# A twelve-layer decoder in one launch: how the attention scores are laid out for the array, who spreads the heads, and two rewritten engine orders

## The reference

```python
x = _layernorm(x + _L0_attn_ref(x, ...))      # linear attention, 16 heads of 8
x = _layernorm(x + _L0_xattn_ref(x, ctx, ...))  # softmax over context and own tokens, 16 heads of 8
x = _layernorm(x + _L0_ffn_ref(x, ...))       # 8 experts and a shared one, SwiGLU
x = _layernorm(x + _L1_attn_ref(x, ...))      # linear attention with decay
x = _layernorm(x + _L1_xattn_ref(x, ctx, ...))  # softmax, 16 heads of 64
x = _layernorm(x + _L1_ffn_ref(x, ...))       # 8 experts, GELU
x = _layernorm(x + _L2_attn_ref(x, ...))
x = _layernorm(x + _L2_xattn_ref(x, ctx, ctx, ...))  # softmax, 16 heads of 8
x = _layernorm(x + _L2_ffn_ref(x, ...))
x = _layernorm(x + _L3_attn_ref(x, ...))      # causal softmax over a latent of 64, 16 heads
x = _layernorm(x + _L3_xattn_ref(x, ctx, ctx, ...))  # mLSTM, 8 heads of 16
x = _layernorm(x + _L3_ffn_ref(x, ...))       # ternary weights
```

## Time and profile before

| | us |
|---|---|
| median of 3 runs | 1021.25 |
| the runs | 1021.25 to 1021.33 |
| the profiled execution, its own time | 1022.06 |
| its span | 1020.0 |
| mean granted clock of TensorE | 0.952 of full speed |

### The profile page before, as it was taken

One profiled execution on the slowest core, in us unless ns is written; L12 is line 12 of the kernel. 1 busy time (PEld: TensorE's weight loads), 2 busy tenths in 40 slices (PEclk: granted clock), 3 DMA queues, 4 the chain that ended last, 5 costly groups with the idle time before them and its releaser, 6 DMA issues. The chain is left out here.

```text
span 1020.0 us, 22561 instructions
## 1 busy us (share of the span) xinstructions
PE 904.2 (89%) x9368; PEld 700.2 (69%) x9368; DVE 539.7 (53%) x1569; ACT 450.7 (44%) x923; POOL 50.8 (5%) x71
## 2 busy tenths in 40 slices
PE   7689899999989998997987979989998989899772
PEld 5257768778778785666556757867887868686441
DVE  5733565653265575347636853655325547454345
ACT  2044343453454673574255233244465446433442
POOL 2300000010010000001000000001001000000000
PEclk8799989999999998999999999999999999999965
DMA  9100000401000301103000000040000030000000
GB/s 344 40 2 3 1 1 1 166 2 37 2 19 1 141 3 40 43 12 139 2 12 1 2 1 2 2 166 33 6 1 19 1 140 1 2 1 2 2 1 21
DMA packets 6838, 36.12 MB, mean 35 GB/s; under 512 B 721, under 2 KB 4305, under 8 KB 5458
## 3 DMA queue, kind: packets, MB, share of 16 engines
q1 hardware_dynamic: 6738, 34.68, 9.1%
HBM read 34.15 MB, written 0.52 MB: 34 GB/s over the span
## 5 line engine op out<-in xcount | busy, mean ns | idle before, releaser
L673 PE MATMUL bank<-xT,weights_F 128*128 128x256 f32 x832 | 202.9, 386 | 3.1 <-ACT p L1818 2.6
L673 PEld LDWEIGHTS bank<-xT,weights_F 128*128 128x128 f32 x832 | 152.0, 193 | 26.8 <-issue 4.2
L681 PEld LDWEIGHTS bank<-weights_F,p 128*128 128x128 f32 x1088 | 133.4, 191 | 18.8 <-DVE p L1363 7.2
L681 PE MATMUL bank<-weights_F,p 128*128 128x128 f32 x1088 | 141.3, 278 | 3.7 <-DVE p L1363 3.0
L1743 ACT ACTIVATE p<-bank 128x512 f32<-128x512 f32 x160 | 84.5, 601 | 121.0 <-PE bank L492 120.9
L1683 ACT ACT_TABLE_LOAD x76 | 97.5, 1283 | 12.9 <-DMA weights_con<-in_con 5.9
L1347 DVE SCALAR_TENSOR_TENSOR res<-bank,comb,res 128x128 f32<-128x128 f32 x184 | 55.7, 345 | 74.1 <-PE bank L681 71.6
L1184 DVE TENSOR_REDUCE m_wide<-bank 128x4 f32<-128x512 f32 x96 | 60.3, 684 | 43.4 <-PE bank L780 33.5
L1818 ACT ACTIVATE p<-bank 128x512 f32<-128x512 f32 x72 | 42.5, 597 | 91.6 <-PE bank L673 91.2
L1363 DVE TENSOR_TENSOR p<-p,bank 128x512 f32<-128x512 f32 x72 | 49.3, 685 | 47.5 <-PE bank L673 27.3
L1894 ACT ACTIVATE p<-bank 128x512 f32<-128x512 f32 x64 | 36.6, 598 | 51.3 <-PE bank L673 51.2
(11 more groups left out here) (319 smaller groups left out, 1356.0 us busy)
## 6 DMA issues: line engine op xcount, KB each, us to landing
weights_F<-in_L1f SPq DMA_DIRECT2D x2, 4096.0 KB, 13.8
weights_F<-in_L0f SPq DMA_DIRECT2D x2, 3456.0 KB, 13.4
weights_F<-in_L2f SPq DMA_DIRECT2D x2, 3456.0 KB, 12.1
weights_Y<-in_L1x_kv SPq DMA_DIRECT2D x2, 1024.0 KB, 10.6
weights_Z<-in_L1x SPq DMA_DIRECT2D x2, 1024.0 KB, 12.9
weights_Y<-in_L2a SPq DMA_DIRECT2D x2, 898.0 KB, 4.4
weights_Z<-in_L2x SPq DMA_DIRECT2D x2, 449.0 KB, 3.2
weights_L3m<-in_L3m SPq DMA_DIRECT2D x2, 288.0 KB, 6.1
```

The source lines that it names most:

```text
L673: m = mm(b[:, k * NT:(k + 1) * NT], W[weight][:, f:f + P], s.xT[:], start=True, stop=True)
L681: m = mm(b[:, tk(u)], h[:, tk(u)], w, start=k == 0, stop=k == len(chunks) - 1)
```

## The change

It has six parts.

1. `bd_k` is gone, and `bd_c` in L0x. The untransposed scores take `bd_q` as weights and the plain keys as the moving side: sixteen products of 32 rows by 128 columns in place of four by 512. DVE's spreading of keys goes from L0a's tail, L0x and L2a; `bd_q` is now made before the first scores of L0x and L2x.
2. In `scores8_t` and L3a's `scores_t` the masks come ahead of the scores.
3. In L1x the maxima are laid out so that a product of 64 rows subtracts them (constant `pick64`).
4. In L3x GpSimd spreads the context `ctxT` into `bd_c`, in L3a already, and the scores take `bd_c` as weights and `xT` as the moving side, eight products of 128 columns in place of two of 512.
5. In L3x PE adds the input gate's term too, by eight more products a call of `units` (constant `choose`, `gates[2]` as the weights), and ACT takes one exponential of 512 columns a bank.
6. `TURN_ORDER` is new on all five engines.

```diff
@@ TURN_ORDER
-        "a15 b1 a3 b2 a1 b1 a1 b1 a1 b2 a1 b2 a3 b2 a7 b2 a1 b1 a2 b1 a5 b1 a1 b2 a1 b1 a1 b3 a1 b2 a1 b3 a1 b1 "
+        "a3 b1 a3 b2 a4 b11 a7 b1 a3 b1 a5 b1 a1 b2 a1 b1 a1 b2 a1 b2 a1 b3 a2 b2 a1 b2 a1 b2 a1 b1 a2 b5 a1 b2 "
...
@@ scores8
-                    for i, b in enumerate(banks):
-                        filled(mm(heads(b[:], 4), s.qT[rows32(i), tk(u)], keys[rows32(i), u], start=mask is None, stop=True),
-                               st, "s", u, blk, i)
+                    for j in range(4):
+                        for i, b in enumerate(banks):
+                            m = mm(b[:, j * T:j * T + T], s.bd_q[rows32(i), u, j], keysT[rows32(i), tk(u)], start=mask is None,
+                                   stop=mask is None or j == 3)
+                            if j == 3:
+                                filled(m, st, "s", u, blk, i)
@@ scores8_t
-                    for i, b in enumerate(banks):
-                        mm(heads(b[:], 4), keysT[rows32(i), tk(u)], s.bd_q[rows32(i), u], start=True, stop=False)
                     if mask is not None:
                         for b in banks:
-                            mm(heads(b[:], 4), ident_bf[:], among(mask, 4), start=False, stop=False)
+                            mm(heads(b[:], 4), ident_bf[:], among(mask, 4), start=True, stop=False)
+                    for i, b in enumerate(banks):
+                        mm(heads(b[:], 4), keysT[rows32(i), tk(u)], s.bd_q[rows32(i), u], start=mask is None, stop=False)
@@ L1x, scores_t
-                                m = less_maximum(u, n, b, j, True)
+                                r, at = n % 2, 4 * (n // 2) + j
+                                m = mm(b[:, j * T:j * T + T], const("pick64")[rows64(r), at:at + 1].to_broadcast([64, P]),
+                                       s.mT[rows64(r), u], start=False, stop=True)
@@ L3x, units
-                        for i, b in zip(both, banks):
-                            u, half = i // 2, i % 2
-                            filled(mm(heads(b[:], 4), s.ctxT[rows64(half), tk(u)], s.bd_c[rows64(half), u], start=True, stop=True),
-                                   "L3x", "s", i)
+                        for j in range(4):
+                            for i, b in zip(both, banks):
+                                u, half = i // 2, i % 2
+                                m = mm(b[:, j * T:j * T + T], s.bd_c[rows64(half), u, j], s.xT[rows64(half), tk(u)], start=True, stop=True)
+                                if j == 3:
+                                    filled(m, "L3x", "s", i)
...
-                                m = mm(b[:, j * T:j * T + T], const("pick")[rows32(u), h:h + 1].to_broadcast([32, P]),
-                                       s.gates[rows32(u), 5], start=False, stop=j == 3)
+                                mm(b[:, j * T:j * T + T], const("pick")[rows32(u), h:h + 1].to_broadcast([32, P]),
+                                   s.gates[rows32(u), 5], start=False, stop=False)
+                                m = mm(b[:, j * T:j * T + T], s.gates[rows32(u), 2], const("choose")[rows32(u), h:h + 1].to_broadcast([32, P]),
+                                       start=False, stop=j == 3)
@@ vector, L0x
                     dve.wait_ge(*freed("L0x", "qk"))
-                    spread_heads(s.bd_k, s.kT, sem("L0x_own_keys"))
+                    spread_heads(s.bd_q, s.qT, sem("queries"))
...
                     pick_maxima("L0x", 0)
-                    yield
-                    spread_heads(s.bd_q, s.qT, sem("queries"))
@@ scalar, L3x
-                    for j in range(4):
-                        o.count(act.activation(s.bd_c[:, :, j], by_sample(s.xT[:]), ACT.Identity,
-                                               scale=const("head16in64")[:, j:j + 1]), sem("L3x_bd") if j == 3 else None)
...
-                        for j in range(4):
-                            cols = slice(j * T, j * T + T)
-                            h = 40 + 4 * (i % 2) + j
-                            o.count(act.activation(s.p[:, i, cols], b[:, cols], ACT.Exp, bias=s.small[:, i // 2, h:h + 1]),
-                                    free("L3x", "D", i) if j == 3 else None)
+                        o.count(act.activation(s.p[:, i], b[:], ACT.Exp), free("L3x", "D", i))
@@ gpsimd, L3a
+                    for u in range(NS):
+                        o.count(pool.tensor_tensor(s.bd_c[:, u], among(s.ctxT[:, tk(u)], 4), over(const("head16in64"), T), ALU.mult),
+                                sem("L3x_bd"))
```

More of the change, by code:

```diff
@@ L323, in __init__ @@
             self.L0a_vo, self.L0a_ctx = w[:, 3328:3584], w[:, 3584:4096].rearrange("p (u d) -> p u d", u=NS)
-            self.bd_c, self.bd_k, self.bd_q, self.kcT = four(0), four(1024), four(2048), w[:, 3072:3328]
+            self.bd_c, self.bd_q, self.kcT = four(0), four(2048), w[:, 3072:3328]
             self.L1a_t1, self.L1a_t2 = (w[:, a:a + 512].rearrange("p (u a d) -> p u a d", u=NS, a=2) for a in (0, 512))
@@ L623, in L0x @@
                     pe.wait_ge(S("masks"), 3)
-                    pe.wait_ge(*told("L0x_ctx_keys"))
-                    scores8("L0x", 0, s.bd_c)
+                    pe.wait_ge(*freed("L0x", "kc"))
+                    pe.wait_ge(*told("queries", NS))
+                    scores8("L0x", 0, s.kcT)
                     yield
-                    pe.wait_ge(*told("L0x_own_keys"))
-                    scores8("L0x", 0, s.bd_k, neg_causal_bf[:], 1)
+                    scores8("L0x", 0, s.kT, neg_causal_bf[:], 1)
                     yield
@@ L631, in L0x @@
                     yield
-                    pe.wait_ge(*told("L0x_ctx_keys"))
-                    scores8("L0x", 1, s.bd_c)
+                    scores8("L0x", 1, s.kcT)
                     yield
-                    pe.wait_ge(*told("L0x_own_keys"))
-                    scores8("L0x", 1, s.bd_k, neg_causal_bf[:], 1)
+                    scores8("L0x", 1, s.kT, neg_causal_bf[:], 1)
                     yield
@@ L639, in L0x @@
                     yield
-                    pe.wait_ge(*told("queries", NS))
                     scores8_t("L0x", 0, s.kcT)
@@ L945, in L2x @@
                     pe.wait_ge(*freed("L2x", "q"))
-                    pe.wait_ge(*told("L2x_keys", NS))
-                    yield from softmax8("L2x", s.bd_k, s.kT)
+                    pe.wait_ge(*freed("L2x", "k"))
+                    yield from softmax8("L2x", s.kT)
                     project("L2x", W["L2x_o"])
@@ L1071, in L3x @@
                     pe.wait_ge(*told("L3x_gates"))
-                    for k, row in enumerate((4, 2)):
-                        m = tr(b[:, 64 * k:64 * k + 64], s.gates[:, row], IDENT[0:64, 0:64])
-                    filled(m, "L3x", "mx")
+                    filled(tr(b[:, 0:64], s.gates[:, 4], IDENT[0:64, 0:64]), "L3x", "mx")
                     yield
-                    pe.wait_ge(*told("L3x_bd"))
+                    pe.wait_ge(*told("L3x_bd", NS))
                     units(0, 3)
@@ L1214, in softmax @@
                     yield
-                    if queries is not None:
-                        spread_heads(s.bd_q, queries, sem("queries"))
-                        yield
                     yield from maxima(st, 1)
@@ L1261, in L0a @@
                         dve.wait_ge(*told("kept"))
-                    def context_keys():
-                        dve.wait_ge(*freed("L0x", "kc"))
-                        spread_heads(s.bd_c, s.kcT, sem("L0x_ctx_keys"))
-                    yield from tail("L0a", s.x_in, context_keys)
+                    yield from tail("L0a", s.x_in)
                 def L0x():
@@ L1546, in L2x @@
                     dve.wait_ge(*freed("L2x", "q"))
+                    spread_heads(s.bd_q, s.qT, sem("queries"))
                     yield
-                    yield from softmax("L2x", s.qT)
+                    yield from softmax("L2x")
                     for u in range(NS):
@@ L1984, in L3x @@
                     b = bank("L3x", "mx")
-                    per_head = lambda k: b[:, 64 * k:64 * k + 64].rearrange("p (u h) -> p u h", u=NS)[:, :, 0:HC]
-                    o.count(act.activation(s.small[:, :, 32:40], per_head(0), ACT.Exp, scale=-1.0))
-                    link(act.copy(s.small[:, :, 40:48], per_head(1)), free("L3x", "mx"))
+                    per_head = b[:, 0:64].rearrange("p (u h) -> p u h", u=NS)[:, :, 0:HC]
+                    o.count(act.activation(s.small[:, :, 32:40], per_head, ACT.Exp, scale=-1.0), free("L3x", "mx"))
                     yield
```

38 lines of the change are left out of this document (18 added, 20 removed), and 55 rows, old and new, of the table TURN_ORDER.

## The result

| | us |
|---|---|
| before, median of 6 runs beside it | 1021.25 |
| the changed kernel, median of 6 runs | 1056.93 (1049.88 to 1059.75) |
| ratio, 95% interval | 1.0326 (1.0286 to 1.0365) |
| the profiled execution, its own time | 1057.23 |
| its span; mean granted clock | 1055.2; 0.947 |

The change made the kernel 3.3% slower. The forecast, 1018.4 in a range to 1028, was wrong in sign and size. Against the profiled execution of before, 35.2 us are to be found.

What follows compares the result with a forecast made beforehand. PE, busy 89% of the span, was taken to bound the kernel. The terms -4.5 - 1.2 + 2 - 4.5 - 2.5 - 1.5 + 4.8 + 4.5 = -2.9 us took the median 1021.25 to 1018.4, range 1009 to 1028.

Steps and rivals of the forecast that it cites:

- the sum: Whole kernel: priced terms add to -2.9 us; new orders left unpriced, a few per cent of 82.5 us waits being 3 us.
- L3x's bias term: L3x: doubled bias products on PE cost +4.8 us in the first turn and +4.5 in the last.
- rival 1: L3x: added products run at half clock at the end and hold every step, giving 1025.7 us; chance 0.18.
- the first turn's +4.8: First-turn L3x: a's two calls add +3.3 us and b's two +1.5; bounds +2 to +6.5.
- the -3.0 for shorter exponentials: Last-turn L3x: one exponential instead of four a bank saves about 1.0 us, three times.
- Rival 2: L0x and L2x: first scores wait 1.3 us for `bd_q`, DVE gives nothing back; +8, 1026.4 us; chance 0.10.
- DVE in the first L0x: First L0x: fewer DVE spreadings shorten PE's two waits of 4.1 us; -4.5 us, bounds -1 to -7.
- rival 4: L1x: equal shapes save nothing and 64-row maxima cost 0.22 us a round; +7.1, 1030.0 us; chance 0.03.
- rival 5: GpSimd's context spreading holds DVE for half of 10.6 us, on the path: 1023.4 us; chance 0.03.
- the +2: L0x and L2x: untransposed scores in sixteen products cost PE +2 us, bounds 0 to +4.
- the -1.5 for ACT: ACT: fewer spreadings, exponentials and table loads; of 10.3 us of table loads, -1.5 us taken, bounds 0 to -4.
- The sign named for a wrong forecast: Forecast wrong if PE's busy time falls, or stretches 70 to 450 and 600 to 960 us move by more than 5.

Runs made afterwards that it cites:

- run 1: The changed kernel's code, parts 1 to 5, with the issue orders of the kernel before: 1032.38 us, ratio 1.0107.
- run 2: The code of the kernel before with the new issue orders, part 6 alone: 1055.25 us, ratio 1.0318.
- run 4: The kernel before with part 5 alone, sixteen bias products a call and one exponential a bank, old orders: 1037.63 us, ratio 1.0166.
- run 10: The kernel before with part 2 alone, masks ahead of the scores, old orders: 1021.77 us, ratio 1.001.
- run 5: The kernel before with part 5 alone, its bias products alternating between the two banks and row groups, old orders: 1021.05 us, ratio 0.9991.
- run 11: The kernel before with part 1 alone, no block-diagonal keys, scores on the queries' spreading, old orders: 1031.97 us, ratio 1.0083.
- run 12: The kernel before with part 4 alone, GpSimd spreading the context, old orders: 1018.72 us, ratio 0.9967.

## Why the prediction was wrong

**The step that failed first** is the last sentence of the sum: the new orders "are unpriced", and "a few per cent of them either way are 3 us". They cost 34 us on the old code and 24.5 on the new (runs 1 and 2). In run 2 PE's idle time grew by 22 us, a quarter of the 82.5 us and not a few per cent. The table decides what stands beside every wait of both streams; that a diff shows it as lines of numbers says nothing of its weight. It should have been a rival with a price, wait by wait: 21 more over 0.6 us make most of those 22 us. Which of them is the order's own, and which follows from another, stays open.

**L3x's bias term.** The price a call was right: +1.79 at full clock (3.42 against 1.63) where +1.63 was said. In the changed kernel the last turn was right too: b's gates to the last product took 21.9 us, under the 24 that would have made rival 1 right; only one of its four calls ran at half. The term that was too small is the first turn's +4.8. In run 4's trace the gate logits of b's first L2f and a's second L0f lie 134.1 us apart instead of 122.9, +11. The four calls between them grew by 7.5 us; the granted clock of the stretch is 0.92 instead of 0.97, and run 10, whose L3x is the old one, has 127.0 us at 0.91 there, so the rest is at least in part the clock. In the last turn of that trace two calls ran at half, the four grew by 11.7, and from b's last gate logits to the end it is 8.4 us more: some 3 came back, as the -3.0 for shorter exponentials has it. (The execution is 4.8 us above its kernel's median.) Nor was it asked whether the products had to follow each other; run 5 shows that the price hangs on this.

**The queries' spreading.** Rival 2 had 0.10. Its +8 counts from the forecast, in which part 1 stands at -5, so it puts part 1 at +3; run 11 measured +8.5, 13.5 above the forecast, with five bare waits of 7.7 us. The mechanism is rival 2's, the size is not. The prediction took the spreading in L2x for 0 (-1 to +2) and priced a gain in the second turn. Its reason, that PE was full there, speaks the other way: where PE is full, DVE's time isn't what it waits for, and 1.3 us of DVE ahead of the first scores is a new wait.

**DVE in the first L0x.** The waits did shrink, 4.1 to 1.6 us, and PE's idle time from 25 us to the first gate logits fell from 14.0 to 12.0 (63.2 us with 51.2 busy, against 64.4 with 50.4). That is 2 instead of 4.5. DVE's relief alone gave none of it: run 1, new code in old orders, has 13.7 us there, and run 2, the new orders alone, 14.1.

**What held.** L1x: -3.4 for -4.5 (-2.8 to -6.1), the call to 0.02 us. So rival 4 is refuted: equal shapes are worth more here than the narrower product. Masks: about nothing for -1.2. The untransposed scores: PE's time for them is 28.7 us in run 11 instead of 29.4, so the +2 wasn't there. GpSimd's spreading took 1.04 us a tile where 1.33 was said. Part 4 was missed by 3.4; that this is ACT's four spreadings, which go out of L3x's beginning, is likely but was not tried by itself.

**GpSimd and DVE.** The prediction's row has DVE lose 0.07 us beside GpSimd. Other rows of the kernel before show more, in both directions:

```profile
308.44 1.64 DVE L1177 TENSOR_TENSOR wide<-qk,weights_con 128x512 f32<-128x512 f32 x2
308.20 0.73 POOL L2037 TENSOR_TENSOR xb<-x_tok,biases 128x256 f32<-128x256 f32 x1 [11.10 <-DVE x_tok L1147]
...
479.74 1.29 DVE L1177 TENSOR_TENSOR wide<-wide,weights_con 128x512 f32<-128x512 f32 x2
479.90 1.71 POOL L2037 TENSOR_TENSOR xb<-x_tok,biases 128x256 f32<-128x256 f32 x1 [10.18 <-DVE x_tok L1147]
```

Where GpSimd began first, DVE's two took 1.64 us instead of 1.3 to 1.4; where DVE began first, GpSimd took 1.71 instead of 0.73. So the exclusion behind rival 5 is real, but its price was not paid: four such cases of 0.36 us stand in the kernel before, none in the changed one (longest 0.81, where the median is 0.68), and run 12 has DVE busy 540.5 us instead of 539.7. (Half of rival 5's 10.6 us on the forecast would be 1023.7, not 1023.4.)

**Together.** 1032.38 of new code in old orders is 14 over the forecast. The single runs miss their terms by more: 7.7 for part 5 (17.0 where 9.3 was said), 13.5 for part 1, 2.2 for the masks, 1.1 for L1x and -3.4 for part 4; with the -1.5 for ACT, of which no run shows anything by itself, that is 22.6. In other words the five parts sum to +19.7 one by one and measured +10.9 together; 9 us don't add up, where the intervals together allow some 7, and no run tells where they are. The other 24.5 are the orders. The sign named for a wrong forecast, the long stretches moving by more than 5, came: b's first L2f is 8.6 us later.

## What to carry to other kernels

A rewritten order of issue can be the largest term of a change, as here: count for both orders what stands beside each short chain, above all where a dense stage gives way to a chain, and give every wait of 1 to 2 us that loses its cover its price. Let small products alternate between row groups and banks; here the same ones cost 17 us in one order and nothing in the other. When an operand is made earlier so that another can go, ask who waits for it where the bounding engine is full. Read the granted clock of each execution before a few microseconds are explained: here the kernels of runs 4 and 5 differ by 18 us at half clock.

## What the runs showed of the hardware that was not expected

- The records of float32 products of 32 rows by 128 columns (two a product) start every 0.11 us when neighbours share a row group and a bank, and every 0.056 us when they alternate between two of each (0.22 us for two and for four records in 4 and 5); eight calls of 32 records take 34.3 and 19.9 us.
- Two kinds of products in turns (`pick` as one operand, `gates` as weights) cost next to nothing for the turns: 3.42 us for 32 records, against 1.63 for sixteen of one kind.
- GpSimd multiplies a 128 x 512 float32 tile in 1.04 us where DVE takes 0.68; half of its 128 x 1024 instruction was 1.33.
- Products of DVE and GpSimd from SBUF hold each other: 1.04 us instead of 0.68 on DVE, 1.71 instead of 0.73 on GpSimd, by who began first.
- All executions of one kernel don't have the same clock: the kernel before shows means of 0.945 to 0.955 beside the runs, with times of 1019.3 to 1028.2 us.
